# A state-space mixer whose projection weight is read in 4 KB pieces during the work, with its norms and its output step written another way

## What is computed

```python
proj = einsum('btd,od->bto', layernorm(x), W_in)          # gate, value_raw, params
value = silu(conv(value_raw))                             # 512 channels
dt, kd = clip(softplus(...)), 0.5 * sigmoid(...)          # per head
bc = einsum('bti,oi->bto', value, W_bc).reshape(B, T, H, 4, N)   # 512 -> 4096
bc = bc / (sqrt(sum(bc * bc, axis=-1)) + 1e-8)            # a norm for each of 4 vectors of 32
# step over t, for each head: z = S * (z - dt*A*s + dt*Bz*u); s = s + dt*z + dt*Bx*u
# y = Cz . z + Cx . s
y = (y + skip * value) * silu(gate)
x = x + einsum('bti,oi->bto', y, W_out)                   # 512 -> 256
```

## Time and profile before

| what | us |
|---|---|
| median of 3 runs | 3144.58 |
| lowest and highest | 3139.78, 3146.74 |
| span of the profiled execution | 3057.5 |
| median less span | 87.1 |
| projections | 0 to 195 |
| mixer, prologue | 195 to 289 |
| mixer, units | 289 to 1974 |
| cross-attention and experts | 1974 to 3057 |

### The profile page before, as it was taken

The page is one execution under the profiler, slowest core; times in us unless marked ns, Lnnn a source line. Parts: engine busy times, 40 slices in busy tenths (PEclk is TensorE's granted clock), DMA queues, the critical chain, the costliest instruction groups (busy, mean ns, idle before and its releaser), DMA issues. The chain is left out here.

```text
span 3057.5 us, 83082 instructions
## 1 busy us (share of the span) xinstructions
PE 2816.9 (92%) x34208; PEld 2144.9 (70%) x34208; DVE 2063.0 (67%) x7110; ACT 1286.8 (42%) x2244; POOL 286.6 (9%) x227
## 2 busy tenths in 40 slices
PE   7965999999999999999999999589879999999998
PEld 3434778778877887787788878533335667888887
DVE  7658999999999999898999999555656201111111
ACT  4634545554454554455455545133324222333332
POOL 0000000000000000000000000000000661333344
PEclk9977999999999999999999999779988999999999
DMA  7874354254435424433542542210006332777776
GB/s 270 233 204 113 80 126 108 64 126 112 102 73 129 108 70 116 112 91 83 124 108 58 135 112 76 69 42 1 1 1 253 109 120 87 197 201 197 197 200 181
DMA packets 249233, 366.15 MB, mean 120 GB/s; under 512 B 57771, under 2 KB 172092, under 8 KB 238140
## 3 DMA queue, kind: packets, MB, share of 16 engines
q1 hardware_dynamic: 226428, 335.99, 39.9%
q0 software_dynamic: 22464, 25.31, 3.9%
HBM read 264.99 MB, written 99.84 MB: 119 GB/s over the span
## 5 line engine op out<-in xcount | busy, mean ns | idle before, releaser
L671 PE MATMUL ring<-valt,wbc 128*128 128x256 f32 x4096 | 947.9, 388 | 31.8 <-DMA valt<-valt_scratch 27.7
L671 PEld LDWEIGHTS ring<-valt,wbc 128*128 128x128 f32 x4096 | 777.4, 194 | 169.0 <-issue 61.5
L824 ACT COPY bc<-ring 128x512 f32<-128x512 f32 x256 | 149.5, 584 | 736.4 <-PE ring L671 736.4
L984 DVE TENSOR_TENSOR uu<-phi,coef 128x64 f32<-128x64 f32 x2048 | 355.1, 211 | 2.1
L990 DVE TENSOR_TENSOR phi<-phi,uu 128x64 f32<-128x64 f32 x2048 | 354.5, 211 | 0.1
L2101 DVE TENSOR_SCALAR f_yr<-fp_y,f_meta 128x256 f32<-128x256 f32 x124 | 54.3, 479 | 423.1 <-PE fp_y L1918 423.1
L729 PE MATMUL yp<-bc,hpad 32*32 32x64 f32 x8192 | 260.2, 289 | 5.0 <-DVE hc L1092 5.0
L729 PEld LDWEIGHTS yp<-bc,hpad 32*32 32x32 f32 x8192 | 225.5, 122 | 50.7 <-issue 50.6
L1985 ACT ACTIVATE f_hT<-fp_h,f_b 128x256 f32<-128x256 f32 x248 | 117.4, 473 | 327.3 <-PE fp_h L1909 327.3
L1918 PE MATMUL fp_y<-f_w,f_hT 128*128 128x256 f32 x992 | 230.7, 386 | 7.9
L1909 PE MATMUL fp_h<-f_xrt,f_w 128*128 128x256 f32 x992 | 225.9, 381 | 0.9 <-ACT f_xrt L1974 0.9
(11 more groups left out here) (227 smaller groups left out, 4006.1 us busy)
## 6 DMA issues: line engine op xcount, KB each, us to landing
f_w<-in_W_dram SPq DMA_DIRECT2D x128, 512.0 KB, 4.2
coef<-par_scratch SPq DMA_DIRECT2D x128, 256.0 KB
fb<-fac_scratch SPq DMA_DIRECT2D x256, 128.0 KB, 3.4
fc<-fac_scratch SPq DMA_DIRECT2D x256, 128.0 KB, 3.8
xg_scratch<-f_fill SPq DMA_DIRECT2D x16, 1032.0 KB, 17.5
f_xr<-xg_scratch SPq DMA_DIRECT2D x64, 258.0 KB, 4.9
vtok_scratch<-p_vtok SPq DMA_DIRECT2D x32, 512.0 KB, 7.9
dub<-vtok_scratch SPq DMA_DIRECT2D x16, 1024.0 KB, 7.3
```

The costliest lines, as they stand in the source:

```text
L671: mm = pe.matmul(ring[:, p % 2, v * UT:(v + 1) * UT], wbc[:, k, g, first + v, :], valt[:, u % 2, k, :], start=(k == 0), stop=(k == 3))
L824: nc.scalar.copy(bc[:, gp, first:first + 2, i // 2, :], o).then_inc(bc_ready, 1)
L984: made[k] = mark(V.tensor_tensor(uu[:, k].rearrange("p i (g b) -> p i g b", b=B), phi[:, t, ::-1, k, :].rearrange("p i (g b) -> p i g b", ...
```

## The change

Three edits, all in the mixer and what leads to it.

1. `wbc` (64 KB in each partition) becomes `wring`, four pieces of 4 KB. A piece holds the weights of one ring slot, 512 KB, laid out so by the host. SP loads the first four pieces in the first stage; from then on ACT issues the load of piece `p + 4` right behind the square of slot `p`, 252 DMAs in all. PE waits for the piece before a slot. A unit has 16 slots, so the whole 8 MB are read once in every unit.
2. `norms` takes the square root as an exponential of half a logarithm (`tiny` keeps the logarithm finite), so four activations stand in place of three, all with functions of one table set, which is loaded once.
3. `outputs` takes 128 tokens as the stationary side: 8 matmuls of 128 x 256 a unit in place of 16 of 64 x 256. The tokens of `xs` lie in another order in the partitions for it, and `load_x` and `store_x` are four DMAs of 64 KB each in place of two of 128 KB.

```diff
-            sp.dma_start(wbc[:], d["W_bc"].rearrange("(k p) (g c o) -> p k g c o", p=P, g=G, c=4)).then_inc(wbc_in, 16)
+            for p in range(WRING):
+                sp.dma_start(wring[:, p], d["W_bc"][p]).then_inc(wbc_in, 16)
...
+WPIECES = 4 * GP
+WRING = 4
...
-        xv = x.rearrange("(q r u s) m -> u r s q m", q=2, r=2, s=L)
+        xv = x.rearrange("(b u q t) m -> u b t q m", b=B, q=2, t=L // 2)
...
             def store_x(u):
                 sp.wait_ge(x1_ready, u + 1)
-                for r in range(2):
-                    sp.dma_start(x1v[u, r], xs[L * r:L * r + L]).then_inc(x_out, 16)
+                for b in range(B):
+                    sp.dma_start(x1v[u, b], xs[b::B]).then_inc(x_out, 16)
...
+                if p >= WRING:
+                    pe.wait_ge(piece_in[p % WRING], 16 * (p // WRING))
                 if p >= 2:
                     pe.wait_ge(sq_ready, p - 1)
                 for v in range(2):
                     for k in range(4):
-                        mm = pe.matmul(ring[:, p % 2, v * UT:(v + 1) * UT], wbc[:, k, g, first + v, :], valt[:, u % 2, k, :],
+                        mm = pe.matmul(ring[:, p % 2, v * UT:(v + 1) * UT], wring[:, p % WRING, k, v, :], valt[:, u % 2, k, :],
                                        start=(k == 0), stop=(k == 3))
...
-                    pe.wait_ge(nr_root, n)
+                    pe.wait_ge(nr_square, n)
...
                 for q in range(2):
-                    for r in range(2):
-                        for k in range(4):
-                            mm = pe.matmul(yp[L * r:L * r + L, q * DM:(q + 1) * DM],
-                                           turns(sg[:, k, :])[:, :, 2 * q + r], wout[:, k, :],
-                                           start=(k == 0), stop=(k == 3), skip_group_check=True)
+                    for k in range(4):
+                        mm = pe.matmul(yp[:, q * DM:(q + 1) * DM], sg[:, k, q * P:(q + 1) * P], wout[:, k, :],
+                                       start=(k == 0), stop=(k == 3), skip_group_check=True)
...
+            nc.scalar.preload_act_table_set("natural_log_exp_and_others")
...
                 nc.scalar.activation(sq[:, p % 2], o, ACT.Square).then_inc(sq_ready, 1)
+                if p + WRING < WPIECES * NU:
+                    act.dma_start(wring[:, p % WRING], d["W_bc"][(p + WRING) % WPIECES]) \
+                        .then_inc(piece_in[p % WRING], 16)
...
-                nc.scalar.activation(nr[:], ssp[:, 0:UT], ACT.Sqrt).then_inc(nr_root, 1)
+                nc.scalar.activation(nr[:], ssp[:, 0:UT], ACT.Ln, bias=tiny[:, 0:1]).then_inc(nr_square, 1)
+                act.wait_ge(nr_square, n + 1)
+                nc.scalar.activation(nr[:], nr[:], ACT.Exp, scale=0.5).then_inc(nr_root, 1)
```

More of the change, by code:

```diff
@@ L28 @@
 EPS_LN, EPS_BC = 1e-5, 1e-8
+SMALLEST = 1e-30
 DT_MIN, DT_MAX, Y_MAX = 1e-4, 0.1, 0.106
@@ L90, with projections @@
 PIDX = {k: i for i, k in enumerate(PRING)}
-def projections(nc, d, x, st, wbc):
+def projections(nc, d, x, st, wring):
     with ExitStack() as ctx:
@@ L198, in _ @@
             sp.wait_ge(raw_out, 32 * NPASS)
-            sp.wait_ge(wbc_in, 16)
+            sp.wait_ge(wbc_in, 16 * WRING)
         @block.tensor
@@ L401, with mixer @@
 UQ = NU // B
-def mixer(nc, d, st, wbc, x, x1):
+WPIECES = 4 * GP
+WRING = 4
+def mixer(nc, d, st, wring, x, x1):
     with ExitStack() as ctx:
@@ L425, in mixer @@
         epsb = sb("epsb", [P, 1])
+        tiny = sb("tiny", [P, 1])
         phi = sb("phi", [P, L + 1, 2, 2, LANES])
@@ L481, in mixer @@
         sums_done = sem("sums_done")
+        piece_in = [sem(f"piece_in{i}") for i in range(WRING)]
+        nr_square = sem("nr_square")
         nr_root = sem("nr_root")
@@ L506, in turns @@
             return v.rearrange("p (t b) -> p t b", b=B)
[L508 to L509 removed]
+        xv = x.rearrange("(b u q t) m -> u b t q m", b=B, q=2, t=L // 2)
+        x1v = x1.rearrange("(b u q t) m -> u b t q m", b=B, q=2, t=L // 2)
         def par(u, q):
@@ L552, in load_x @@
             def load_x(u):
-                for r in range(2):
-                    sp.dma_start(xs[L * r:L * r + L], xv[u, r]).then_inc(x_in, 16)
+                for b in range(B):
+                    sp.dma_start(xs[b::B], xv[u, b]).then_inc(x_in, 16)
             def store_x(u):
                 sp.wait_ge(x1_ready, u + 1)
-                for r in range(2):
-                    sp.dma_start(x1v[u, r], xs[L * r:L * r + L]).then_inc(x_out, 16)
+                for b in range(B):
+                    sp.dma_start(x1v[u, b], xs[b::B]).then_inc(x_out, 16)
             def store_factors(n):
@@ L642, in _ @@
                 if u > 0:
-                    sp.wait_ge(x_out, 32 * u)
+                    sp.wait_ge(x_out, 16 * B * u)
                     load_x(u)
@@ L652, in _ @@
             store_x(NU - 1)
-            sp.wait_ge(x_out, 32 * NU)
+            sp.wait_ge(x_out, 16 * B * NU)
         @block.tensor
@@ L926, in _ @@
             V.memset(hpad[:], 0.0)
+            V.memset(tiny[:], SMALLEST)
             V.memset(one[:], 1.0).then_inc(set_ready, 1)
@@ L1097, in residual @@
                 dve.wait_ge(o_full, u + 1)
-                dve.wait_ge(x_in, 32 * (u + 1))
+                dve.wait_ge(x_in, 16 * B * (u + 1))
                 V.tensor_tensor(xs[:], yp[:].rearrange("p (q m) -> p q m", q=2), xs[:], ALU.add).then_inc(x1_ready, 1)
@@ L1154, in attention @@
         ("valt", (NU, P, 4, UT), F32), ("par", (UQ, 5, P, UT), F32), ("fac", (NU * GP, P, UT), F32))}
-    with nc.sbuf_tensor("wbc", [P, 4, G, 4, P], F32) as wbc:
-        projections(nc, d, x, st, wbc)
-        mixer(nc, d, st, wbc, x, x1)
+    with nc.sbuf_tensor("wring", [P, WRING, 4, 2, P], F32) as wring:
+        projections(nc, d, x, st, wring)
+        mixer(nc, d, st, wring, x, x1)
 SK, DC = 77, 192
@@ L2129, in layouts @@
     w = np.asarray(inputs["L0_attn_W_bc"]).reshape(G, J, 4, N, DI)[..., chan]
-    r["W_bc"] = w.transpose(0, 2, 1, 3, 4).reshape(H * 4 * N, DI).T
+    w = w.transpose(0, 2, 1, 3, 4).reshape(WPIECES, 2, P, 4, P)
+    r["W_bc"] = w.transpose(0, 4, 3, 1, 2)
     r["W_out"] = np.asarray(inputs["L0_attn_W_out"]).T[chan]
```

1 line of the change is left out of this document (removed).

## The result

The changed kernel takes 3228.31 us (median; 3219.48 to 3239.25) where the kernel before takes 3142.76 (3139.78 to 3146.74): ratio 1.0261, 95% interval 1.0235 to 1.0287. It is slower by some 85 us; the forecast was 9 us slower, and its range ended at 3184.

The account below looks back on a forecast made before the run. DVE's loop of 101.2 us plus the `fb` round trip was taken to bound most units. Units +4.5, prologue +5, tail -0.3 made +9.2 us: span 3066.7 plus 87.1 gave 3154 us, range 3124 to 3184.

Parts of the forecast that it names:

- The frame: Mixer units: DVE's own loop of 101.2 us plus the `fb` round trip sets most units; PE adds a little in some.
- the ring on the DMA engines, `fb` 2: Group 2's `fb` load: two pieces ahead make it 0 to 2.6 us later, taken as 2.0; wait 0.5 becomes 2.5.
- `fb` 3: DVE's `fb` wait at group 3: 2.63 us of a drained queue plus 0.5 for pieces running over, 3.1 a unit.
- The ring on PE and ACT: Mixer: pieces asked for four slots ahead arrive in time for PE; ACT has room for 16 issues a unit. No cost.
- DVE's waits for PE: Mixer units: fall from 0.8 to 0.2 us, since PE is 1.2 us sooner and DVE 2 us later: -0.6.
- Norms: Mixer: the norm, ready 3.4 us sooner, removes DVE's 0.75 us wait a unit; gain counted at 0.3, between 0 and 0.75.
- Output step: Mixer `outputs`: 4.87 to 3.65 us, 1.2 a unit on PE, nearly hidden; removes at most 0.8 of DVE's waits.
- Prologue: Before the units: four pieces beside the parameters' store delay DVE's start by 0 to 6.5 us, taken as 5.
- Tail: Mixer's end: last `outputs` 1.6 us shorter, extra `load_x` and `store_x` issues 1.3 longer: -0.3 us.
- The contention is larger than its bound: Mixer: pieces also slow `coef`, `fb` 4 us late at group 2 and 4.39 at group 3: 3181; within the forecast's 0.58.
- The instructions of PE come late: Mixer: PE's stops, if instruction loads meeting DMA traffic, spread to the other three groups: +3.6 us a unit, 3208; chance 0.11.
- The pieces ride free: Mixer: two queues fill DMA gaps, neither `fb` wait grows, 1.1 us a unit is gained: 3129; chance 0.28.

Follow-up runs that it names:

- resident kernel: The changed kernel with all 16 weight pieces kept in SBUF and none read again, other two edits kept: 3141.96 us, ratio 0.9965 to the kernel before.
- two_later: The changed kernel with a ring of eight, the pieces behind group 0's first two squares asked for in group 2: 3198.46 us, ratio 1.0137 to the kernel before.
- norms alone: The changed kernel with all pieces kept in SBUF and the output step and x transfers as before the change: 3152.38 us, ratio 1.0015.
- outputs alone: The changed kernel with all pieces kept in SBUF and the norms as before the change: 3142.83 us, ratio 0.9991.
- second profile: The kernel before, unchanged, run once more for another profile: 3154.9 us, span 3153.0.
- spread12: The changed kernel, ring of twelve loaded in the first stage, pieces asked for singly in groups 1 to 3, in the prologue only at its end: 3131.08 us, ratio 0.9943.
- later: The changed kernel, ring of eight, no pieces in group 0 or behind group 1's first two squares, then two per square through group 2, one in group 3: 3208.89 us.
- spread: The changed kernel, ring of eight, pieces singly in groups 1 to 3, none in group 0 or behind group 1's first two squares: 3139.61 us, ratio 0.9985.

## Why the prediction was wrong, step by step

*The frame was right.* DVE's loop of 101.2 us and the `fb` round trip on top of it set the unit, before and after; the budget closes to 0.2 us in twelve profiles.

*The step that failed: the ring on the DMA engines, `fb` 2.* The prediction asked when the load of `fb` would come if two pieces lay ahead of it, and bounded that by 2.6 us, of which it took 2.0. Measured against the resident kernel it is 4.8 (5.53 less 0.71). The round trip has two transfers in a row, a store that must land before the load is issued, and only the load was costed. The store lands 3.7 us later by itself, the load 1.2 us, and the "upper bound" of 2 x 1.63 less 0.6 was a bound for one passage alone. two_later shows it: the two pieces beside the store, taken away, bring the wait from 5.53 to 0.90, the load's part with the store's.

*`fb` 3.* Set at 2.63 + 0.5 = 3.1; measured 4.70. The idea that a late `fb` 2 drains the queue for `fb` 3 held for one unit of before, when nothing else filled the queue. With the pieces of groups 0 and 1 the DMA engines are full from 1088 to 1116 us (share 0.95 and 1.01 in the rows above), and both waits grew, this one by the load alone. `fc`, put at nothing, waits 0.5. So DVE's waits are 10.7 us a unit where 5.8 were forecast (5.6 for `fb`, 0.2 for PE); 4.9 us in 15 units are 74 us, which is what the time missed the forecast by.

*The ring on PE and ACT.* As forecast: PE waits for no piece, and an issue takes ACT 0.33 to 0.37 us. The 1.3 us at the upper end of the prediction's reading are two issues together (x2 in the earlier trace rows); nothing hung on it.

*DVE's waits for PE.* Forecast: 0.8 to 0.2 us a unit, 0.6 gained. Measured 0.01: right, but because DVE is later than forecast. `outputs` takes 3.72 us a unit, forecast 3.65.

*Norms.* The wait for the norm is gone, as forecast. The gain of 0.3 us a unit is not there (106.95 with norms alone). The prediction gave a reason itself, that the store then meets the DMA burst, and should have followed it to zero; that this is the whole reason is not shown.

*Output step.* The prediction read its gain as at most DVE's 0.8 us of waits for PE. With outputs alone a unit is 1.0 us shorter than in the first profile of before, about as much. What it did not see is that PE's stops fall with it, from 36.6 to 14.3 us, though nearly as many instruction blocks land. Why they do is open.

*Prologue.* Forecast: DVE's wait 12.6 to 17 us, 5 us on the path. Measured 18.69, against 12.64 and 12.86 in the second profile: 5.8 to 6.1 us. The wait is right, a little low; spread12 takes it back. On the path it is less: DVE comes to this wait at 227.4 us, in the two profiles of before at 231.2 and 228.2, and leaves it 2.3 and 5.1 us later than there. So the first stage, forecast at 0, did not become longer.

*Tail.* Forecast -0.3; from the fifteenth `residual` to the sixteenth it is 59.86 us, before 59.82 and 58.75. Nothing to see.

*The sum.* The 87.1 us between span and median were taken as lying around the span. They lie in it: 96 us in the experts, which the first profile of before lacks and the second has; span and time differ by 2 us in every other run. It did no harm, since both kernels have that stretch, but it was a difference of two executions, not a constant.

*The rivals.* "The contention is larger than its bound" (3181) was the right one, and also too small: it gave `fb` 2 four microseconds and `fb` 3 its 4.39, where 5.53 and 4.70 came, and it made +2 us a unit of them, though its own terms (4 + 4.39 less the 4.7 of today) are 3.7. "The instructions of PE come late" (3208, at 0.11) came near the time for the wrong reason: PE's stops did double, from 36.6 to 81.1 us in 14 units, but in the changed kernel DVE does not wait for them. They cost DVE time in later and two_later (4.2 and 2.2 us a unit). "The pieces ride free" was refused by the changed kernel, and yet spread is that case: the free DMA time is there, only not where the change asked for it.

By the Trainium skill (DMA: Bandwidth & Descriptors, Issuing engines are not separate DMA queues) DMAs of ACT and of SP interleave on the same engines, with no gain but issue time. The traces agree: two pieces beside the store delay it by 3.7 us.

By the Trainium skill (Runtime: NRT & Kernel Launch, Instruction fetch mechanics) crossing a block of instructions costs one DMA kick, mostly hidden. The traces agree for most blocks, not for all: 196 land in the 14 units of the changed kernel, and 22 of PE's stops there are longer than 0.9 us, up to 5.7; all stops together come to 81 us.

## What to carry to other kernels

Cost a store that must land before a load as two passages, each beside what is in flight on other queues too, and look at what stands right before the store: two transfers out of sixteen, moved away, took back nearly all of the extra wait at group 2 (5.53 to 0.90 us), since a store that lands late also sends the load into later traffic. The places of extra traffic can be worth more than its amount: the same 8 MB cost 6.0 us a unit or nothing here. Where PE stops between matmuls that wait for nothing, look for a block of instructions that lands just before it goes on. The twelve profiles have nearly the same number of such blocks, and stops of 11 to 91 us in 14 units: it is not their number that makes the difference.

## What was not expected of the hardware

In the experts PE falls for about 100 us into single matmuls, most of them 2.1 to 2.8 us apart, while POOL issues its scatters (the first profile of before has the scatters without it); PE in the second profile of before, in order of time:

```profile
2420.92 0.38 PE L1826 MATMUL fp_y<-f_ws,f_hT 128*128 128x256 f32 x1 [2.43 <-issue]
2423.05 0.59 PE L1826 MATMUL fp_y<-f_ws,f_hT 128*128 128x256 f32 x1 [1.75 <-issue]
2425.15 0.59 PE L1826 MATMUL fp_y<-f_ws,f_hT 128*128 128x256 f32 x1 [1.51 <-issue]
```

In the changed kernel no block of PE's instructions lands between 2482 and 2610 us, the time of this stretch there, where one comes about every 35 us otherwise; then PE is at its old pace. That a refill was missed and PE fetched its instructions one by one is an explanation that fits, but it was not tested. The stage after the mixer is 85 to 102 us longer in every profile of this study than in the first one of before; that is as much as the change costs.
